# Attention and a two-of-sixteen expert layer on one core: pieces of weight loads, a scatter without its hold, and a refilled drain

## The reference

```
x = x + attn(layernorm(x), ctx, ctx, lens)     # 16 heads of 16, keys beyond lens masked, then @ Wo
u = layernorm(x)
s = softmax(u @ centroids.T + expert_biases)
topk_vals, topk_idx = top_k(s, 2)
routed = sum over the two chosen e of s_e * (u @ Wr[e].T + br[e])
shared = (sum_e u @ Ws[e].T + sum_e bs[e]) / 2
out = x + u + routed + shared
```

## Time and profile before

| | us |
|---|---|
| median of 3 runs | 255.09 (253.17 to 255.13) |
| time of the profiled execution | 253.09 |
| its span, first to last instruction | 251.3 |
| mean granted TensorE clock in it | 0.939 |
| PE busy | 224.2 (89% of the span) |
| DVE, ACT, POOL busy | 158.3, 95.7, 136.2 |

### The profile page before, as it was taken

The page is one execution under the profiler, slowest core; times in us unless marked ns, Lnnn a source line. Parts: engine busy times, 40 slices in busy tenths (PEclk is TensorE's granted clock), DMA queues, the critical chain, the costliest instruction groups (busy, mean ns, idle before and its releaser), DMA issues.

```text
span 251.3 us, 5129 instructions
## 1 busy us (share of the span) xinstructions
PE 224.2 (89%) x1547; PEld 189.6 (75%) x1547; DVE 158.3 (63%) x501; ACT 95.7 (38%) x243; POOL 136.2 (54%) x235
## 2 busy tenths in 40 slices
PE   7999899999998899999989999997977997765594
PEld 3768789888888788989879787875865885553483
DVE  2896978888888898898854475855622422220460
ACT  2243466647646566565534121412311422200012
POOL 7110322545565745676575640688888888883000
PEclk9999999999999999999977599997997999989689
DMA  5999999999984112121121124767776312102995
GB/s 155 365 406 270 317 357 373 340 382 405 434 353 158 54 51 100 64 93 63 60 105 64 45 84 109 194 199 243 204 220 197 102 60 74 68 0 40 413 357 192
DMA packets 20314, 48.80 MB, mean 194 GB/s; under 512 B 5059, under 2 KB 13765, under 8 KB 18888
## 3 DMA queue, kind: packets, MB, share of 16 engines
q1 hardware_dynamic: 12912, 31.97, 38.2%
q0 software_dynamic: 5376, 12.50, 13.4%
q10 hardware_dynamic: 2000, 4.01, 4.4%
HBM read 23.22 MB, written 46.29 MB: 277 GB/s over the span
## 4 chain that ended last, share of the span: by engine, by line
PE 63%; POOL 11%; DMA 10%; DVE 6%; issue 6%; ACT 1%; POOLq 0%; ACTq 0%; DVEq 0%
PE O L971 10%; POOL y L620 7%; PE T L890 6%; DMA lists<-urow,pos 6%; PE B L930 5%; PE S L980 5%; PE B L1043 4%; PE A L890 4%; PE S L942 4%; PE A L1155 3%; PE S L890 3%; PE T L1155 3%; PE B L1155 3%; PE O L1155 3%; POOL passed_x L627 2%
## 5 line engine op out<-in xcount | busy, mean ns | idle before, releaser
L575 POOL DMA_INDIRECT lists<-urow,pos x32 | 32.9, 1027 | 33.1 <-PE S L942 21.4
L519 ACT ACTIVATE uTl<-S 128x256 f32<-128x256 f32 x47 | 17.6, 384 | 53.6 <-PE S L890 41.7
L434 ACT ACTIVATE pT<-T 128x512 f32<-128x512 f32 (+1 forms) x48 | 25.2, 525 | 19.7 <-PE T L890 17.6
L971 PE MATMUL O<-vfront,pT 128*128 128x34 f32 x256 | 30.2, 274 | 0.0
L971 PEld LDWEIGHTS O<-vfront,pT 128*128 128x128 f32 x256 | 30.0, 192 | 0.2
L890 PE MATMUL T<-const,s_sb 128*128 128x128 f32 (+1 forms) x160 | 25.9, 277 | 2.2 <-ACT pT L434 1.7
L720 DVE TENSOR_REDUCE rowmax<-S 128x16 f32<-128x1232 f32 x16 | 23.0, 1440 | 6.2 <-PE S L942 6.2
L460 ACT ACTIVATE urow<-x,shift,rstds 128x256 f32<-128x256 f32 x32 | 18.9, 595 | 16.5 <-POOL shift L590 11.6
L890 PEld LDWEIGHTS T<-const,s_sb 128*128 128x128 f32 (+1 forms) x160 | 19.4, 141 | 5.2 <-issue 3.5
L620 POOL DMA_INDIRECT y<-yrow,padblock x16 | 16.0, 1001 | 11.0 <-DVE yrow L868 8.6
L735 DVE SCALAR_TENSOR_TENSOR s_sb<-S,rstds,scaledmax 128x1024 f32<-128x1024 f32 (+1 forms) x26 | 21.0, 850 | 0.0
(11 more groups left out here) (211 smaller groups left out, 481.9 us busy)
## 6 DMA issues: line engine op xcount, KB each, us to landing
lists<-padblock SPq DMA_DIRECT2D x5, 2056.0 KB, 18.0
padblock<-lists SPq DMA_DIRECT2D x32, 128.5 KB
wr<-in_wrT SPq DMA_DIRECT2D x1, 4096.0 KB
br<-in_br SPq DMA_DIRECT2D x1, 2048.0 KB
wr<-y SPq DMA_DIRECT2D x4, 512.0 KB, 8.4
wr<-y ACTq DMA_DIRECT2D x4, 512.0 KB, 8.6
urow<-lists SPq DMA_DIRECT2D x15, 128.5 KB
x<-in_x SPq DMA_DIRECT2D x1, 1024.0 KB
```

The source lines that it names most:

```text
L434: nc.scalar.activation(pT[t % 2][0:rows, c0:c1, :], T[0:rows, 0:c1 - c0, :], ACT.Exp).then_inc(p_ready, 1)
L575: nc.gpsimd.indirect_dma_start(out=lists, out_offset=bass.IndirectOffsetOnAxis(ap=pos[:, t, c:c + 1], axis=0), in_=urow[t % NR][c][:, :], ...
L971: last = M(to, pT[t % 2][0:v.shape[0], c, :], v.rearrange("p h j -> p (h j)"), start=(c == 0), stop=(c == CH - 1), skip_group_check=True)
```

## The change

- `lens` is loaded by SP, ahead of `wq`, and no longer by ACT ahead of the constants.
- `wr` is loaded in 8 pieces of 512 KB and `br` in 2 of 1 MB. Each piece waits for one more tile to have its attention output taken (`out_taken` 5 to 14).
- `scatter_rows` no longer waits for the scores of tile s + 2 (`s_psum`).
- At step s = 15 POOL does `scale_second(14)` ahead of the scatter of tile 12, not behind it.
- `shared_weights` is cut into three parts, done at s = 0, 1 and 2.
- At s = 15 PE multiplies the identity with `wo` into a bank that nobody reads, ahead of line 1068. In the drain the halves of `shared(0)` and `shared(1)` are moved to earlier places.
- For lists 0 and 1, `list_stepped` is also raised directly behind the multiplication, so that DVE's bias add need not wait for the transposes behind it; the counts in `flipped` and `multiplied` follow.

```diff
+WPIECES, BPIECES, PIECES_FROM = 8, 2, 5
+WSR_STEPS = 4
...
-            return k + 1 if k < AHEAD else max(k, AHEAD + 1)
+            return {0: 1, 1: 2, 2: 4, 3: 6, 4: 6}.get(k, k + 2)
...
-            return AHEAD + k
+            return {0: 3, 1: 5}.get(k, k + 5)
...
+            load(lens[:, :], lens_in.rearrange("(o b) -> o b", o=1).to_broadcast([P, BATCH]), "len")
...
-            load(wr[:, :, :], wrT_in.rearrange("(c p) n -> p c n", p=P), "wr")
-            load(br[:, :], br_in.rearrange("(o e) n -> o (e n)", o=1).to_broadcast([P, EXPERTS * D]), "br")
+            w = EXPERTS * D // WPIECES
+            for j in range(WPIECES):
+                sp.wait_ge(out_taken, PIECES_FROM + j)
+                load(wr[:, :, j * w:(j + 1) * w], wrT_in[:, j * w:(j + 1) * w].rearrange("(c p) n -> p c n", p=P), "wr")
+            w = EXPERTS // BPIECES
+            for j in range(BPIECES):
+                sp.wait_ge(out_taken, PIECES_FROM + WPIECES + j)
+                load(br[:, j * w * D:(j + 1) * w * D], br_in[j * w:(j + 1) * w, :].rearrange("(o e) n -> o (e n)", o=1)
+                     .to_broadcast([P, w * D]), "br")
...
-                if is_tile(s + 2):
-                    pool.wait_ge(s_psum, s + 3)
...
-                if TILES - 1 <= s <= TILES:
+                if s == TILES:
                     scatter_rows(s - 3, s)
...
                 elif s == TILES - 1:
+                    for c in range(DC):
+                        M(idle_bank, ident, wo[:, c, :], start=(c == 0), stop=(c == DC - 1))
...
             rank(t - 2)
+            pe.wait_ge(wsr_ready, WSR_STEPS)
+            shared(0, (0,))
             pe.wait_ge(o_ready, TILES)
...
-            pe.wait_ge(wsr_ready, 1)
+            shared(0, (1,))
             rank(t - 1)
...
-            shared(0)
+            shared(1, (0,))
             pe.wait_ge(lastT_ready, 1)
...
-            shared(1)
+            shared(1, (1,))
             shared(2)
...
+                if k < 2:
+                    last.then_inc(list_stepped, 1)
```

More of the change, by code:

```diff
@@ L411, in _ @@
         def _(act):
-            act.dma_start(lens[:, :], lens_in.rearrange("(o b) -> o b", o=1).to_broadcast([P, BATCH])).then_inc(arrived["len"], 16)
             act.dma_start(const[:, 0:NFIRST], const_in[:, 0:NFIRST]).then_inc(arrived["const"], 16)
@@ L614, in _ @@
                     scale_second(s - 1)
-                if is_tile(s - 3) and not TILES - 1 <= s <= TILES:
+                if is_tile(s - 3) and s != TILES:
                     scatter_rows(s - 3, s)
@@ L703, in value_block, with shared_weights @@
                                 .to_broadcast([RESTROWS, OCTS, HEADS // OCTS, DH]), ALU.mult).then_inc(vblock_ready, 1)
-            def shared_weights():
-                dve.wait_ge(arrived["ws"], 16 * SHARED)
-                dve.wait_ge(arrived["bsr"], 16)
-                link(V.tensor_tensor(wsr[:, :, :], ws[:, 0, :, :], ws[:, 1, :, :], ALU.add))
-                link(V.tensor_tensor(brow[:, :], bsr[:, 0, :], bsr[:, 1, :], ALU.add))
-                link(V.tensor_scalar(wsr[:, :, :], wsr[:, :, :], 1.0 / SHARED, None, ALU.mult))
-                V.tensor_scalar(brow[:, :], brow[:, :], 1.0 / SHARED, None, ALU.mult)
-                for c in range(DC):
-                    last = V.tensor_tensor(wsr[:, c, c * P:(c + 1) * P], wsr[:, c, c * P:(c + 1) * P], ident, ALU.add)
-                last.then_inc(wsr_ready, 1)
+            def shared_weights(part_of):
+                if part_of == 0:
+                    dve.wait_ge(arrived["ws"], 16 * SHARED)
+                    dve.wait_ge(arrived["bsr"], 16)
+                    V.tensor_tensor(wsr[:, :, :], ws[:, 0, :, :], ws[:, 1, :, :], ALU.add).then_inc(wsr_ready, 1)
+                    V.tensor_tensor(brow[:, :], bsr[:, 0, :], bsr[:, 1, :], ALU.add).then_inc(wsr_ready, 1)
+                elif part_of == 1:
+                    dve.wait_ge(wsr_ready, 2)
+                    V.tensor_scalar(wsr[:, :, :], wsr[:, :, :], 1.0 / SHARED, None, ALU.mult).then_inc(wsr_ready, 1)
+                    V.tensor_scalar(brow[:, :], brow[:, :], 1.0 / SHARED, None, ALU.mult)
+                else:
+                    dve.wait_ge(wsr_ready, 3)
+                    for c in range(DC):
+                        last = V.tensor_tensor(wsr[:, c, c * P:(c + 1) * P], wsr[:, c, c * P:(c + 1) * P], ident, ALU.add)
+                    last.then_inc(wsr_ready, 1)
             def find_max(t):
@@ L831, in _ @@
                     dve.wait_ge(arrived["ebias"], 16)
-                if s == 1:
-                    shared_weights()
+                if 0 <= s <= 2:
+                    shared_weights(s)
                 if s == TILES + 1:
@@ L861, in _ @@
             dve.wait_ge(table_ready, 1)
-            dve.wait_ge(arrived["br"], 16)
+            dve.wait_ge(arrived["br"], 16 * BPIECES)
             for k in range(LISTS):
@@ L1136, in _ @@
             pe.wait_ge(table_ready, 1)
-            pe.wait_ge(arrived["wr"], 16)
+            pe.wait_ge(arrived["wr"], 16 * WPIECES)
             def list_transposes(k):
```

## The result

The changed kernel took 266.86 us (median of 4 runs, 264.79 to 267.69), the kernel before 255.11 us beside it. The ratio is 1.047, 95% interval 1.039 to 1.055. It is slower by 11.8 us; the forecast was 248.6, with 252.2 as the upper end. The profiled execution took 266.5 us with a span of 264.7 us (251.3 before).

The account below looks back on a forecast made before the run. Bound by PE to 128 us, a PE, DVE and ACT chain to 155, then POOL's scatters to 227.82. 253.09 - 1.7 - 0.5 - 0.4 - 2.5 = 248.0, plus 0.6 allowance: 248.6 us, range 246.2 to 252.2.

Parts of the forecast that it names:

- Lifting the hold on scatters is worth nothing elsewhere: Steady tiles: removing the scatters' wait for scores gains nothing in other tiles, since POOL is not late there; 0 us.
- The rival for this side: POOL's earlier scatter slows DVE's `rden` and `o_sb`, up to 0.8 us in each of 12 tiles: 258.2 us; chance 0.04.
- The sum: All gains taken from the profiled 253.09 us give 248.0; an added 0.6 makes the forecast 248.6 us.
- Scatters and pieces: Tiles from 56.85 to 95.61 us: weights in pieces end the waits for `urow`; 1.7 us gained, between 0 and 2.5.
- Shared weights: Start, near s = 1: three parts on DVE spare PE a wait for `o_sb`; 0.5 us gained, between 0 and 0.8.
- `lens`: Start: constants issue about 0.45 us earlier, `wq` and context one issue later; taken as 0, 0.4 either way.
- First bias: First list: DVE adds the bias without waiting for PE's transposes; 0.4 us gained, between 0 and 0.8.
- the same 69.4 us: List stage: POOL's 47 scatters to `y` were to take as long as before, 69.4 us.
- The drain: End of tiles to first list load: filling PE's work and fewer clock falls gain 2.5 us; bounds 4.0 gained, 1.5 lost.
- the fall that was to stay: Drain: the clock's fall at 128.4 us stays, since nothing fills that gap; only the one at 135.1 goes.
- that the clock could stay up: Drain: no fall of the clock at all, 1.5 us more gained: 247.1 us; chance 0.14.
- the reason that I gave for the fall at 128.4 us: Drain: the clock fell in the 0.84 us in which PE was idle up to 128.57 us.

Follow-up runs that it names:

- e15: Changed kernel, row scatters unheld, `lens` back on ACT's queue, last loads of `x` and `xT` exchanged; 265.57 us, ratio 1.045.
- e16: e15 with the row scatters again held until the scores of tile s + 2; 250.04 us, ratio 0.981.
- e1: Changed kernel with the row scatters again held until the scores of tile s + 2; 247.18 us, ratio 0.979.
- e5: Changed kernel, nothing edited, measured again in another session; 247.08 us, ratio 0.980.
- e9: Changed kernel, nothing edited, measured once more in a further session; 245.85 us, ratio 0.980.
- e12: e3 run again in another session: changed kernel with scatters held and `lens` on ACT's queue; 246.37 us, ratio 0.981.
- e4: Kernel before with only `wr` and `br` loaded in pieces, scatters still held; 248.57 us, ratio 0.987.
- e7: Changed kernel with `wr` and `br` loaded whole again, scatters unheld; 246.57 us, ratio 0.980.
- e3: Changed kernel with the scatters held again and `lens` back at the head of ACT's queue; 245.85 us, ratio 0.976.
- e11: Kernel before with the drain's edits alone; 248.21 us, ratio 0.990.
- e2: Kernel before with only the hold on the row scatters removed; 252.43 us, ratio 0.982.
- e6: Kernel before with the hold on scatters removed and the weights loaded in pieces; 249.63 us.
- e10: Changed kernel with the filler page's transfer held until the scores of the tile in hand and `lens` on ACT's queue; 247.95 us.
- e17: Same program as e10 (filler page held, row scatters unheld, `lens` on ACT's queue), in a late session; 256.44 us, ratio 1.015.
- e18: Changed kernel with `lens` on ACT's queue and the filler page's transfer issued ahead of the row scatters, not behind them; 261.82 us, ratio 1.031.

## Why the prediction was wrong

**The step that failed** is the sentence "Lifting the hold on scatters is worth nothing elsewhere", with the rival beside it. It asked which wait of POOL's the hold makes, and not over which of the other engines' signals POOL's transfers would come to lie. In the measurement it costs 10 x 1.55 = 15.5 us; e15 and e16, which differ by the hold alone, show 15.7 us for the same stretch in another late session. The chance given to a slower kernel was 0.04, and that for another mechanism. In prompt sessions the step is right: 247.2 us with the hold (e1), 247.1 and 245.9 without (e5, e9).

**The rival for this side** was near the place and wrong in the mechanism. It had POOL's first scatter slow DVE's `rden` and `o_sb` down, by up to 0.8 us in 12 tiles, and argued from the earlier trace rows that a scatter over these two does no harm. That holds still: `o_sb` takes 0.42 us after the change. What suffers is the signal of PE during the second and third transfer, to DVE and to ACT. The trace of before had it, by 0.38 to 0.52 us in seven of its last eight tiles; timeline:

```profile
63.12 1.16 PE L930 MATMUL B<-xT,wqc 128*128 128x128 f32 x8
63.81 1.00 POOL L603 DMA_INDIRECT lists<-padblock,run_i  x1 [0.31 <-issue]
64.69 0.38 ACT L441 ACTIVATE qT<-B 128x256 f32<-128x256 f32 x1 [1.08 <-PE B L930]
```

PE's queries end at 64.28, and ACT starts 0.41 us later, where other signals take 0.03 to 0.07. In a prompt session the same pair is 0.03 us apart (e12, 64.35 and 64.38). Asking what would happen if the transfers moved onto a signal without slack would have given a rival at 248.6 + 10 x 0.4 = 252.6 at least; its true size, 1.55, was not to be read there.

**The sum was right where signals are prompt.** e5 and e9 give 0.980 of the kernel before; of the profiled 253.09 us that is 248.0, and the sum said 248.0. That it agrees so closely is partly luck. `lens` was taken as 0 and cost over 1 us at the start, and the drain's filling was worth its 2.5 us, or more, by another course of the clock than the one forecast. Term by term:

- *Scatters and pieces*, 1.7 us: 1.64 us of waits are gone from the tiles in the profile after (1.63 in e4). That it is the pieces was only half right: without the hold they are worth nothing (e7 246.6, e5 247.1). e4 as a whole gained 3.2 us; the rest lies in its drain, where its clock fell less than in the earlier trace rows, and I can't tell why. (The list loads come 28 us after 124 us, not 20; nothing hangs on that.)
- *Shared weights*, 0.5: the third and the fourth period fell from 7.39 and 7.59 us to 7.08 and 7.31, so 0.59.
- *`lens`*, 0 with 0.4 either way: it costs 1.3 us between e1 and e3, but nothing is left of it between e9 and e12, where a fall of the clock in the drain took it back. The range was worked out from the time of an issue, about 0.45 us; the landing of the context moved by more than that.
- *First bias*, 0.4: the first add starts 0.45 us behind PE's multiplication in the kernel before (156.78 and 157.23) and 0.13 us behind it in the changed one (169.34 and 169.47), so 0.3 us. The forecast that the same 69.4 us follow failed in the late session, where they were 71.5.
- *The drain*, 2.5: e11 gives 2.6, with one fall of the clock. The size is right, the course isn't: the fall that was to stay was the one at 128.4 us, and e11's lies at 136.3 to 139.7. In the late session the drain gained 3.95, with none; that the clock could stay up was one of the rivals. And some of the gain comes without any filling, as e2, e4 and e6 show.

On the clock, the reason that I gave for the fall at 128.4 us doesn't carry. The gap ahead of the transposes of `o_sb` is still there, 0.81 us at 145.34 in the changed kernel, and the granted clock stays at 1.00 through it, as it does through the 1.3 us in which PE is idle in each tile from 84 us on. Two executions of one program differ (e5 falls in the drain, e9 doesn't), which is what the Trainium skill, "TensorE: Matmul & The Clock Gate", section "What's actually happening", lets expect.

**What stays open.** What makes a session late isn't settled. It isn't the program (e10 and e17 are the same one, 247.95 and 256.44 us as medians, tiles of 7.40 and 8.20 us), and the number of the chip doesn't tell it: sessions 4 and 5 both report number 14, without saying whether it was the same machine. That signals are late and records of updates missing in the same three sessions, and in no other, may mean that the recording of the profile holds the signals up, or that both suffer from one cause; every execution here has its span and clock recorded, so none tells what an unrecorded one takes. That GpSimd's transfers hold the signals up is shown by moving them (e15 to e18), but not by what: their issuing, the data that they move, or their own updates. Nor was a single transfer over a signal, with none ahead of it, tried.

**The version to keep** holds the scatters, loads the weights in pieces, fills the drain, and leaves `lens` on ACT's queue: e3 and e12, 0.976 and 0.981 of the kernel before where signals are prompt. Where they are late, only e16 has the hold, with the two loads exchanged besides: 0.981, and 0.984 by the medians of all executions. So the hold is what was faster in both kinds of session; e3's exact form wasn't run in a late one.

## What to carry to other kernels

Ask of a wait that is to be taken out not only who gains by it, but which instructions it keeps apart: here it kept GpSimd's transfers away from the signal of TensorE that DVE's chain waits for. Where a profile shows a consumer starting 0.4 us after its producer and all others 0.05, look what stands over it, even if nobody waits for it now. And repeat a surprising result in another session, with the kernel before beside it, ahead of explaining it by the code.

## What was not expected of the hardware

- Indirect transfers issued by GpSimd back to back delayed TensorE's semaphore updates by 0.85 us (one of them over the signal) and 1.5 to 1.65 us (two), in three of seven sessions; the two signals held up then arrived within 0.04 us of each other. In the other four VectorE started 0.07 us after the scores, with the same instructions in the same places.
- With one transfer of 1 KB put ahead of it on its queue, a transfer of 154 KB landed 5.7 to 6.1 us after its own issue in all traces; without it, 4.6 or 4.7 us (5.2 in e12).
- A gap of 0.84 us on TensorE went with a fall of the granted clock to 0.50 in the kernel before. In the changed one a gap of 0.81 us went with none, nor did gaps of 1.3 us in each of seven tiles and one of 1.99 us at 56.90, though one of 1.64 us at 65.80 did. The fall in e5's drain costs 1.1 us against e9's.
- The same 47 indirect transfers, issued by GpSimd one after the other, took 68.2 to 68.5 us in the traces of prompt sessions and 69.4 to 71.7 us in those of late ones.
